# Two groups of denominator sums placed directly ahead of the key transposes in the first stage of a linear-attention and gated-FFN layer

## The chip, the cores and the metric

The kernel runs on one core of one Trainium2 chip. The metric is device time in microseconds for one execution. The engines are called PE (TensorE, with PEld for its weight loads), DVE (VectorE), ACT (ScalarE), POOL (GpSimd) and SP (SyncE, which issues the DMAs). They run in parallel, each through its own fixed queue of instructions, and meet at semaphores.

## What is computed

The input x has 4096 tokens of 512 numbers. One layer is computed, in fp32:

```python
q, k, v = x @ Wq.T, x @ Wk.T, x @ Wv.T      # 16 query heads, 4 key/value heads, 128 wide
q, k = rope(q), rope(k)
qf, kf = elu(q) + 1, elu(k) + 1
# over the tokens, for each head
state = state + kf[:, None] * v[None, :];  z = z + kf
o = (qf @ state) / (qf . z + 1e-6)
x = layernorm(x + o @ Wo.T)
x = layernorm(x + ffn(x))    # two Walsh-Hadamard transforms around a gated FFN of width 2048
```

## The kernel before

The first stage (projections and linear attention, about the first 930 us) is the only one that the change touches. It walks over 8 tiles of 512 tokens. In each tile there are 4 groups (one key head and its 4 query heads) and 4 chunks of 128 tokens. The later stages (output projection with the first layer norm, then the FFN) are left as they are.

Each engine's work in a tile is written out by hand as a list of events: one letter and two digits. A prime means that the event belongs to the next tile, so the tiles overlap. `ORDER_*` (L44 to L75) is the list of a tile in a loop over 6 tiles, run once more ahead of it as "first", `START_*` fills the pipeline and `LAST_*` (L183 to L198) is the last tile. The events that matter here:

- PE: `Jgc` projects one head (c = 0 is the key of group g, 1 to 4 its queries) with 12 matmuls of 512 columns (L626). `Vc` projects values. `Dg` sums the products q·z of a group over the partitions with a matrix of ones (L650, four fp32 matmuls that show as 8 records, each in its own quarter of the columns). `Tg` transposes the key of group g (L644, fp32). `Cgc` is the scores of a chunk (L657, 3 matmuls of 512 columns), `Zgc` adds to the state (L664, 3 matmuls of 128 columns), `Ugc` forms the numerators of a chunk (L677 and L680, 6 matmuls of 512 columns). Apart from D and T, the operands are split in two fp32r parts.
- ACT: `S` (the rotated copy, L1006 and L1007), `X` (exp, L1010), `L` (upper part of q or k, L1016), `A` (of the scores, L1036), `N` (of the state, L1041), `K` (of the transposed key, L1025), `O` (numerators out of their bank, L1045), `H` (of x, L1032).
- DVE: `M` (times cosine, L1310), `R` (rotation summed, L1314), `E` (elu + 1, L1322; after it the projection's bank is free), `Q` (running sum of the keys, L1328), `P` (q times z, L1336; it writes the four tiles `pr` that D reads), `Y` (copies D's bank out, L1361), and the lower parts `A`, `N`, `K`, `H`, `W`.
- POOL: `I` (times sine, L1482), `L` (lower part of q or k, L1485), `G` (the causal mask on the scores, two selects, L1492).
- SP: `O` stores a chunk's numerators (L1687), `Y` a group's sums (L1692), `B` loads a piece of x (L1678).

J, V, T and D share three PSUM banks, `pj0` to `pj2`, dealt out in the order in which these jobs stand in PE's list:

```python
JOBS = [e for e in EVENTS["PE"] if e[0] in "JVTD"]
def job_bank(kind, a, b=0):
    return [e[:3] for e in JOBS].index((kind, a, b)) % NB      # NB = 3
```

`jobs_before` (L164) finds the last job of the same bank and `released` (L593) waits for the step that empties it: for J that is `f_done` of its E, for V `v_lo`, for T `t_lo` (K on DVE), for D `den_free` (Y on DVE). Before the change, the jobs around D2 get these banks: J32 2, J33 0, J34 1, D2 2, J00' 0, T3 1, J01' 2, J02' 0, J03' 1. So J01' waits for Y2, and J02' for E00'.

Further waits that the steps below use: P31 waits for D2 (`dn_done`, since D2 reads `pr`); D2 for the four P of group 2; Z for N; N for the Z before; C30 for L34 on POOL; O on ACT for the store of the numerators two units back (`num_out`), because there are two buffers `no`; Y on SP for Y on DVE. On SP the tile's list is `... O20 B2' Y2 B0' O21 O22 O23 ...`, on ACT it is `... O21 O22 L34 S00' K3 N30 O23 A30 X00' S01' ...`.

Of the kernel before, what the change touches and what calls it, by code (L numbers as in the profile page):

```python
# [42 lines left out]

ORDER_PE = """  # L44
J21 U03 C11 C12 Z10 J22 J23 J24 Z11 U10 C13 U11 D1 J30 Z12 J31 C20 U12 Z13 C21 T2 U13 J32 J33 Z20 J34 Z21 C22
U20 U21 C23 D2 Z22 U22 J00' Z23 T3 U23 C30 J01' Z30 C31 C32 J02' J03' U30 J04' Z31 U31 V0' Z32 J10' Z33 C33 V1'
C00' T0' C01' U32 U33 D3 J11' J12' Z00' U00' J13' Z01' J14' U01' V2' V3' C02' C03' Z02' J20' D0' Z03' T1' U02'
C10'
"""

# [7 lines left out]

ORDER_DVE = """
N10 R20 A10 P12 E20 P13 M21 P14 R21 N11 A11 E21 Q2 M22 R22 M23 E22 R23 M24 E23 R24 N12 A12 P21 E24 A13 Y1 P22  # L60
M30 N13 P23 R30 P24 M31 A20 R31 E30 K2 E31 N20 A21 Q3 M32 R32 M33 N21 E32 R33 H0' M34 H1' A22 N22 H2' R34 E33 Y2
H3' A23 E34 N23 P31 P32 P33 M00' K3 N30 P34 R00' A30 E00' Q0' M01' A31 R01' N31 E01' M02' R02' M03' A32 E02'
R03' M04' E03' N32 R04' W0' N33 E04' M10' A33 R10' W1' E10' K0' A00' N00' A01' P01' Y3 P02' P03' M11' P04' R11'
Q1' E11' N01' M12' R12' M13' E12' N02' R13' M14' E13' R14' W2' E14' W3' A02' A03' N03' Y0' P11' K1' M20'
"""
# [117 lines left out]

LAST_PE = """
J21 U03 C11 C12 Z10 J22 J23 J24 Z11 U10 C13 U11 D1 J30 Z12 J31 C20 U12 Z13 C21 T2 U13 J32 J33 Z20 J34 Z21 C22
U20 U21 C23 D2 Z22 U22 Z23 T3 U23 C30 Z30 C31 C32 U30 Z31 U31 Z32 C33 U32 Z33 U33 D3
"""

LAST_DVE = """
N10 R20 A10 P12 E20 P13 M21 P14 R21 N11 A11 E21 Q2 M22 R22 M23 E22 R23 M24 E23 R24 N12 A12 P21 E24 A13 Y1 P22  # L190
M30 N13 P23 R30 P24 M31 A20 R31 E30 K2 E31 N20 A21 Q3 M32 R32 M33 N21 E32 R33 M34 A22 N22 R34 E33 Y2
A23 E34 N23 K3 N30 A30 A31 N31 P31 P32 A32 N32 N33 A33 P33 P34 Y3
"""

LAST_POOL = """
# [1626 lines left out]
```

## Time and profile before

| | us |
|---|---|
| median of 3 runs | 2302.26 (2300.16 to 2302.41) |
| the profiled execution | 2300.89 |
| its span, first to last instruction | 2299.1 |
| ACT busy | 1273.6 (55%) |
| POOL busy | 1128.5 (49%) |
| mean granted TensorE clock | 0.995 |

Seven of the 8 tiles have a J01' in their list: the "first" tile and the six of the loop. Their D2 begin at 122.9, 234.6, 345.6, 457.3, 568.9, 680.6 and 791.6 us, so a tile takes about 111.5 us. The last tile's D2 begins at 903.5 us.

How to read the rows: a line of the timeline has the start and the duration in us, the engine, the line of the kernel, the operation, output<-inputs, the shape and how many instructions were merged; brackets hold the idle time before it and what ended it. Matmul records overlap: one of 512 columns lasts 0.39 us, while the next starts 0.23 us later at the full clock. So starts are compared with starts.

### The profile page before, as it was taken

What the parts mean: (1) busy time and instruction counts of PE and PEld (TensorE: products, weight loads), DVE (VectorE), ACT (ScalarE), POOL (GpSimd) and SP (SyncE); (2) the same over time, 40 slices, a digit from 0 to 9 for tenths busy, and PEclk for the clock granted to TensorE, in tenths of its full rate; (3) what the DMA queues carried; (4) which work ended last, traced back from release to release, by engine and by line L of the source; (5) the groups of instructions that cost most, each with busy time, mean ns of one, the idle gap of its engine ahead of it and who ended that gap; (6) DMA issues with size and microseconds to landing.
All of it is one profiled execution on the core that took longest, in us unless ns stands there. A gap on an engine that the chain in (4) does not pass through costs nothing.

```text
span 2299.1 us, 32686 instructions
## 1 busy us (share of the span) xinstructions
PE 2255.0 (98%) x10226; PEld 1826.7 (79%) x10226; DVE 1827.3 (79%) x2479; ACT 1273.6 (55%) x2285; POOL 1128.5 (49%) x1007
## 2 busy tenths in 40 slices
PE   8899999999999999999999999999999999999998
PEld 6678787787878787788888778888888888888887
DVE  6777777778786868888888897787888788878877
ACT  6666666666666767233444455454545544554543
POOL 5667676767676767455544733321342133303321
PEclk9999999999999999999999999999999999999999
DMA  4011201111110215777778541323223322222323
GB/s 158 33 65 38 70 35 66 43 63 56 45 69 32 73 35 198 264 254 256 251 243 269 184 131 56 123 84 113 82 94 97 115 88 92 92 83 83 102 64 101
DMA packets 132710, 252.87 MB, mean 110 GB/s; under 512 B 44576, under 2 KB 45344, under 8 KB 122880
## 3 DMA queue, kind: packets, MB, share of 16 engines
q1 hardware_dynamic: 132608, 251.60, 32.7%
q8 instruction: 53, 0.87, 0.2%
q14 instruction: 49, 0.40, 0.1%
HBM read 188.11 MB, written 63.44 MB: 109 GB/s over the span
## 4 chain that ended last, share of the span: by engine, by line
PE 71%; issue 11%; POOL 10%; DVE 5%; ACT 2%; DMA 0%; POOLq 0%; ACTq 0%; DVEq 0%; SPq 0%
PE pj L626 16%; PE pj L709 10%; PE pnum L709 6%; PE pj L723 5%; PE psc L709 5%; PE pst L709 4%; PE psc L723 4%; PE pj L636 3%; PE pnum L723 3%; PE psc L657 3%; PE pnum L677 3%; PE pnum L680 3%; PE pst L723 2%; POOL fa L1415 1%; POOL fb L1416 1%
## 5 line engine op out<-in xcount | busy, mean ns | idle before, releaser
L1445 POOL TENSOR_TENSOR wcs<-wcr 128x256 f32<-128x256 f32 x64 | 67.8, 1060 | 514.7 <-DVE wcl L1187 504.3
L1482 POOL TENSOR_TENSOR tb<-tb,sinb 128x512 f32<-128x512 f32 x160 | 223.4, 1396 | 82.4 <-ACT tb L1007 82.1
L626 PE MATMUL pj<-xah,wqh 128*128 128x512 f32 x504 | 200.3, 397 | 4.0 <-DVE Kf L1322 2.4
L1485 POOL TENSOR_TENSOR Ql<-tb,Qh 128x512 fp32r<-128x512 f32 x128 | 170.9, 1338 | 66.9 <-ACT Qh L1016 66.9
L547 PE MATMUL pj<-woh,oh 128*128 128x512 f32 x512 | 202.1, 395 | 0.0
L547 PE MATMUL pj<-woh,ol 128*128 128x512 f32 x512 | 200.0, 391 | 0.0
L547 PE MATMUL pj<-wol,oh 128*128 128x512 f32 x512 | 199.8, 390 | 0.0
L626 PE MATMUL pj<-xah,wql 128*128 128x512 f32 x504 | 197.1, 391 | 0.0
L626 PE MATMUL pj<-xal,wqh 128*128 128x512 f32 x504 | 197.0, 391 | 0.0
L1310 DVE TENSOR_TENSOR pj<-pj,cosb 128x512 f32<-128x512 f32 x157 | 109.1, 695 | 77.8 <-ACT tb L1007 77.3
L1492 POOL TENSOR_SCALAR_AFFINE_SELECT Ah<-Ah 128x512 fp32r<-128x512 f32 x128 | 101.3, 792 | 113.9 <-DVE Al L1351 113.2
L709 PE MATMUL pj<-xch,wch 128*128 128x512 f32 x384 | 151.3, 394 | 5.7 <-DVE xcl L1193 3.8
L1006 ACT ACTIVATE tb<-pj 64x512 f32<-64x512 f32 x157 | 93.6, 596 | 111.0 <-PE pj L626 109.2
L709 PE MATMUL pj<-xcl,wch 128*128 128x512 f32 x384 | 150.6, 392 | 0.0
L709 PE MATMUL pj<-xch,wcl 128*128 128x512 f32 x384 | 150.4, 392 | 0.0
L1336 DVE TENSOR_TENSOR pr<-tb,zc 128x512 f32<-128x512 f32 x128 | 139.0, 1100 | 1.0 <-PE pj L650 1.0
L1314 DVE SCALAR_TENSOR_TENSOR pj<-pj,tb 128x512 f32<-128x512 f32 x157 | 108.8, 693 | 32.1 <-POOL tb L1482 31.0
L1010 ACT ACTIVATE tb<-pj,minus 128x512 f32<-128x512 f32 x157 | 108.3, 690 | 42.0 <-DVE pj L1314 40.4
L1398 POOL TENSOR_TENSOR rstd<-ve,neghalf 128x1 f32<-128x1 f32 x32 | 40.4, 1262 | 182.1 <-DVE ve L1078 182.1
L626 PEld LDWEIGHTS pj<-xah,wqh 128*128 128x128 f32 x504 | 95.3, 189 | 31.2 <-issue 5.9
L1258 DVE SCALAR_TENSOR_TENSOR tha<-tha,ga 128x512 f32<-128x512 f32 x64 | 53.6, 837 | 80.8 <-ACT tha L952 80.7
L922 ACT ACTIVATE wdh<-wdr 128x512 fp32r<-128x512 f32 x123 | 77.1, 627 | 69.0 <-PE pj L723 34.8
(291 smaller groups left out, 7110.2 us busy)
## 6 DMA issues: line engine op xcount, KB each, us to landing
num_scratch<-no SPq DMA_DIRECT2D x128, 256.0 KB, 2.4
nt<-num_scratch SPq DMA_DIRECT2D x32, 1024.0 KB, 5.5
rb<-rden_scratch SPq DMA_DIRECT2D x32, 1024.0 KB, 6.8
wdr<-wd_scratch SPq DMA_DIRECT2D x128, 256.0 KB, 3.2
wcr<-in_wg SPq DMA_DIRECT2D x64, 256.0 KB, 2.7
wcr<-in_wu SPq DMA_DIRECT2D x64, 256.0 KB, 3.1
xst<-in_xT SPq DMA_DIRECT2D x34, 256.0 KB, 3.8
xr<-in_x SPq DMA_DIRECT2D x32, 256.0 KB, 5.6
```

The lines of the kernel that those rows point to most:

```text
L547: last = nc.tensor.matmul(py[s][:, :], a[s][:, h, :], b[:, h, :], start=(h == 0 and i == 0), stop=(h == H - 1 and i == 2))
L626: last = nc.tensor.matmul(bank[:, :], w[:, b, :], x[:, b, :], start=(k == 0), stop=(k == 11))
L709: last = nc.tensor.matmul(bank[:, :], a[n % 2][:, w, c, :], b[i][:, c, :], start=(start and k == 0), stop=(k == 5), skip_group_check=True)
L723: last = nc.tensor.matmul(result_banks(k)[t][:, :], a[:, tok], b[:, :], start=(f == 0 and i == 0), stop=(f == FB - 1 and i == 2))
L1006: nc.scalar.activation(tb[c][0:64, :], bank[64:128, :], ACT.Copy)
L1010: nc.scalar.activation(tb[c][:, :], jobs_at[bank_index("J", g, c, where)][:, :], ACT.Exp, bias=minus1[:, 0:1]).then_inc(exp_done, 1)
L1310: nc.vector.tensor_tensor(bank[:, :], bank[:, :], cosb[:, :], ALU.mult).then_inc(cos_done, 1)
L1314: nc.vector.scalar_tensor_tensor(out=bank[:, :], in0=bank[:, :], scalar=1.0, in1=tb[c][:, :], op0=ALU.add, op1=ALU.add).then_inc(rot_done, 1)
L1336: nc.vector.tensor_tensor(pr[c - 1][:, :], tb[c][:, :], zc[:, :], ALU.mult).then_inc(z_product, 1)
L1482: nc.gpsimd.tensor_tensor(tb[c][:, :], tb[c][:, :], sinb[:, :], ALU.mult).then_inc(sin_done, 1)
L1485: nc.gpsimd.tensor_tensor(Ql[g % 2][:, c, :], (tb[c] if c else Kf)[:, :], f32(Qh[g % 2][:, c, :]), ALU.subtract).then_inc(lo_done, 1)
L1492: ins = nc.gpsimd.affine_select(out=a[:, :, :], in_=a[:, :, :], compare_op=ALU.is_ge, fill=0.0, base=0, pattern=[[0, G], [1, CH]], channel ...
```

## The change

In every tile D2 moves behind Z22, U22, J00' and Z23, to stand directly ahead of T3, and D0' moves behind Z03', to stand directly ahead of T1'. DVE's Y2 moves behind H3', A23, E34 and N23, since D2 now follows Z23, which needs N23. SP's, ACT's and POOL's lists stay.

```diff
 ORDER_PE
-U20 U21 C23 D2 Z22 U22 J00' Z23 T3 U23 C30 J01' Z30 C31 C32 J02' J03' U30 J04' Z31 U31 V0' Z32 J10' Z33 C33 V1'
-C00' T0' C01' U32 U33 D3 J11' J12' Z00' U00' J13' Z01' J14' U01' V2' V3' C02' C03' Z02' J20' D0' Z03' T1' U02'
+U20 U21 C23 Z22 U22 J00' Z23 D2 T3 U23 C30 J01' Z30 C31 C32 J02' J03' U30 J04' Z31 U31 V0' Z32 J10' Z33 C33 V1'
+C00' T0' C01' U32 U33 D3 J11' J12' Z00' U00' J13' Z01' J14' U01' V2' V3' C02' C03' Z02' J20' Z03' D0' T1' U02'
 C10'
 ORDER_DVE
-M30 N13 P23 R30 P24 M31 A20 R31 E30 K2 E31 N20 A21 Q3 M32 R32 M33 N21 E32 R33 H0' M34 H1' A22 N22 H2' R34 E33 Y2
-H3' A23 E34 N23 P31 P32 P33 M00' K3 N30 P34 R00' A30 E00' Q0' M01' A31 R01' N31 E01' M02' R02' M03' A32 E02'
+M30 N13 P23 R30 P24 M31 A20 R31 E30 K2 E31 N20 A21 Q3 M32 R32 M33 N21 E32 R33 H0' M34 H1' A22 N22 H2' R34 E33
+H3' A23 E34 N23 Y2 P31 P32 P33 M00' K3 N30 P34 R00' A30 E00' Q0' M01' A31 R01' N31 E01' M02' R02' M03' A32 E02'
 LAST_PE
-U20 U21 C23 D2 Z22 U22 Z23 T3 U23 C30 Z30 C31 C32 U30 Z31 U31 Z32 C33 U32 Z33 U33 D3
+U20 U21 C23 Z22 U22 Z23 D2 T3 U23 C30 Z30 C31 C32 U30 Z31 U31 Z32 C33 U32 Z33 U33 D3
 LAST_DVE
-M30 N13 P23 R30 P24 M31 A20 R31 E30 K2 E31 N20 A21 Q3 M32 R32 M33 N21 E32 R33 M34 A22 N22 R34 E33 Y2
-A23 E34 N23 K3 N30 A30 A31 N31 P31 P32 A32 N32 N33 A33 P33 P34 Y3
+M30 N13 P23 R30 P24 M31 A20 R31 E30 K2 E31 N20 A21 Q3 M32 R32 M33 N21 E32 R33 M34 A22 N22 R34 E33
+A23 E34 N23 Y2 K3 N30 A30 A31 N31 P31 P32 A32 N32 N33 A33 P33 P34 Y3
```

The order of the shared-bank jobs changes with it, from `J34 D2 J00' T3 J01' J02'` to `J34 J00' D2 T3 J01' J02'`. The code deals the banks out anew: J00' gets bank 2 and D2 bank 0. The start's list has `Z03 D0 T1` already and stays; the swap of D0' and Z03' leaves the order of the jobs as it was.

## Rows read from the trace of the kernel before

**Rows 1.** The page's first part, busy time and share of each engine.
```profile
PE 2255.0 (98%) x10226; PEld 1826.7 (79%) x10226; DVE 1827.3 (79%) x2479; ACT 1273.6 (55%) x2285; POOL 1128.5 (49%) x1007
```
**Rows 2.** Who waited for whom, PE, 72 to 900 us: total us, times, longest.
```profile
PE pnum L677 <- POOL Al L1492: 4.3, 7, 0.6
```
**Rows 3.** Timeline of PE around D2 of a middle tile (start us, duration us).
```profile
457.26 1.06 PE L650 MATMUL pj<-pr,onesd 128*32 128x512 f32 x8
458.26 0.33 PE L664 MATMUL pst<-Vh,Kth 128*128 128x128 f32 x1
...
459.43 0.47 PE L677 MATMUL pnum<-Ah,Vh 128*128 128x512 f32 x1 [0.62 <-POOL Al L1492]
...
460.89 0.39 PE L626 MATMUL pj<-xah,wkh 128*128 128x512 f32 x1
...
463.61 0.22 PE L664 MATMUL pst<-Vh,Kth 128*128 128x128 f32 x1
...
463.89 0.63 PE L644 MATMUL pj<-identb,Kf 128*128 128x128 f32 x4
464.28 0.47 PE L677 MATMUL pnum<-Ah,Vh 128*128 128x512 f32 x1
...
466.22 0.50 PE L657 MATMUL psc<-Qh 128*128 128x512 f32 x1 [0.32 <-POOL Ql L1485]
...
467.02 0.39 PE L626 MATMUL pj<-xah,wqh 128*128 128x512 f32 x1
```
**Rows 4.** Timeline of DVE, the same tile: Y2, P31 to P33, M00', R00', E00'.
```profile
459.32 0.68 DVE L1361 COPY dn<-pj 128x512 f32<-128x512 f32 x1
...
462.41 2.61 DVE L1336 TENSOR_TENSOR pr<-tb,zc 128x512 f32<-128x512 f32 x3
465.63 0.70 DVE L1310 TENSOR_TENSOR pj<-pj,cosb 128x512 f32<-128x512 f32 x1 [0.61 <-ACT tb L1007]
...
467.89 0.68 DVE L1314 SCALAR_TENSOR_TENSOR pj<-pj,tb 128x512 f32<-128x512 f32 x1
...
469.33 0.69 DVE L1322 SCALAR_TENSOR_TENSOR Kf<-tb,pj 128x512 f32<-128x512 f32 x1 [0.17 <-ACT tb L1010]
```
**Rows 5.** Timeline of SP's queue, the same tile: Y2, then the numerators from O21.
```profile
460.16 0.60 SPq L1692 DMA_DIRECT2D den_scratch<-dn  x1
...
461.94 22.30 SPq L1687 DMA_DIRECT2D num_scratch<-no  x5
```
**Rows 6.** Timeline of ACT, the same tile: O22.
```profile
463.26 0.60 ACT L1045 ACTIVATE no<-pnum 128x512 f32<-128x512 f32 x1 [2.22 <-DMA num_scratch<-no]
```
**Rows 7.** Line L1687 (numerator stores), 450 to 470 us.
```profile
DMA to landing us min/median/max: 2.4/3.3/4.4
```
**Rows 8.** Timeline of PE where it resumes after idle time, in the first 115 us.
```profile
55.37 0.45 PE L664 MATMUL pst<-Vh,Kth 128*128 128x128 f32 x1 [4.29 <-DVE Sl L1356]
...
61.27 0.50 PE L626 MATMUL pj<-xah,wqh 128*128 128x512 f32 x1
...
108.10 0.50 PE L626 MATMUL pj<-xah,wqh 128*128 128x512 f32 x1 [2.41 <-DVE Kf L1322]
...
112.41 0.53 PE L626 MATMUL pj<-xah,wqh 128*128 128x512 f32 x1
```
**Rows 9.** Windows: busy of each engine (count), granted clock, DMA share, GB/s.
```profile
58.00:60.00 2.00, 2.00 (x7) 1.52 (x6) 0.00 (x0) 0.60 (x1) 0.00 (x0) 0.50 0.00 0
```
**Rows 10.** Timeline of PE in the start, where D0 stands directly ahead of T1.
```profile
69.92 1.06 PE L650 MATMUL pj<-pr,onesd 128*32 128x512 f32 x8
70.91 0.66 PE L644 MATMUL pj<-identb,Kf 128*128 128x128 f32 x4
```
**Rows 11.** Timelines: PE D0', DVE Y0' of the tile before; POOL I00'.
```profile
410.62 1.07 PE L650 MATMUL pj<-pr,onesd 128*32 128x512 f32 x8
...
411.84 0.69 DVE L1361 COPY dn<-pj 128x512 f32<-128x512 f32 x1 [2.66 <-PE pj L650]
...
466.13 1.28 POOL L1482 TENSOR_TENSOR tb<-tb,sinb 128x512 f32<-128x512 f32 x1
```

## The prediction

> **What bounds the kernel now.** I read the busy shares first: PE is busy 98% of the span [rows 1], the other engines at most 79%. Then the waits of PE in the stretch of the seven full tiles: the only one that comes in every tile is one of 0.6 us for POOL (7 times, 4.3 us) [rows 2], and at C30 there is one of 0.3 us in some of them [rows 3]. So in this stage a microsecond put on PE, or a wait put before it, is a microsecond of the result, and there are only about 0.9 us a tile in which a move could hide. Then the timelines of one middle tile on each engine, around D2. The reader is to see in [rows 3] which of PE's waits are there already: U22 (459.43) waits 0.62 us for POOL's mask, C30 (466.22) waits 0.32 us for POOL's L34, and J01' (467.02) starts without a wait. In [rows 4]: DVE does P31 to P33 right behind N23, and finishes E00' at 469.33 + 0.69 = 470.02, which is 3.0 us after J01' has started. All seven tiles show this pattern.
>
> **The gain that is there.** D and T are the only fp32 jobs among fp32r ones, and the first matmul behind either is longer: 0.33 us for Z behind D against 0.22 us for Z behind a projection, and 0.47 us for U behind T against the usual 0.39 us [rows 3]. So a D or a T costs about 0.1 us on the way out. Directly ahead of T, as the start has it, D's way out is gone; D takes 70.91 - 69.92 = 0.99 us, as it does now (458.26 - 457.26 = 1.00), and T lasts 0.66 instead of 0.63 us [rows 10, 3]. So a pair saves 0.11 - 0.03 = 0.08 us. There are 8 pairs D2, T3 and 7 pairs D0', T1': 15 x 0.08 = 1.2 us at most, 0.05% of the time. (On the way in I take both places as equal.)
>
> **D0' behind Z03'.** PE is not made to wait: N03' is done long before: on DVE it stands ahead of Y0', and DVE idles 2.66 us between them [rows 11]. D0' and Y0' come 0.28 us later (Z03' takes 0.28 us, as 463.61 to 463.89 shows), and with them P11' and K1' on DVE. The next user of the bank, J21, has T1', U02' and C10' ahead of it, 0.4 + 9 x 0.23 = 2.4 us behind D0' (a step of 512 columns is (463.61 - 460.89) / 12 = 0.23 us, rows 3), and Y0', which starts 411.84 - 410.62 = 1.22 us after D0' and takes 0.7 us, ends 1.9 us after D0' begins, so 0.9 us after D0' is through. That is covered. Cost nothing, gain 7 x 0.08 = 0.6 us.
>
> **D2 behind J00' and Z23: PE's own time.** U22 does not start earlier because D2 is gone from before it. Its releaser is POOL's mask, which hangs on A22 and not on D2, so U22 stays at 459.43, J00' at 460.89 and Z23 at 463.61 [rows 3]. The gap that D2 filled is left empty. Behind Z23 (0.28 us) and 0.1 us for the way in, which T behind Z doesn't show and I grant D, D2 starts at 463.61 + 0.38 = 463.99, T3 at 464.98, U23 at 465.39, and C30 six steps and T's 0.1 us later, at 465.39 + 1.46 = 466.85. The 0.32 us wait for L34, with its re-entry, is absorbed. J01' could start at 466.85 + 3 x 0.23 = 467.53, 0.51 us later than now. That includes the saving at T3.
>
> **D2 behind J00' and Z23: the DVE queue.** Y2 is queued on DVE behind N23 and ahead of P31. Y0' shows that the copy starts 1.22 us after its D [rows 11]. So Y2 starts at 463.99 + 1.22 = 465.21, and P31 at 465.81, where it started at 462.41 [rows 4]. (P31 would have waited for D2 in any case.) DVE idles about 3.4 us there. Behind P31 are queued P32, P33, M00', K3, N30, P34, R00', A30 and E00'. From P31's start to E00's end the row shows 470.02 - 462.41 = 7.61 us, of which 0.61 was a wait that now is over by then. So E00' ends at 465.81 + 7.0 = 472.8.
>
> **The new wait.** Before the change nobody on PE needed E00' before J02', which stands 3 + 12 + 6 matmuls behind (Z30, J01', C31, C32), some 4 us after J01' starts. But the banks are dealt by the order of the jobs, and J00' and D2 have swapped: J01' now takes the bank of J00'. That bank is released by E00', not by Y2. J01' is ready at 467.53 and may start at 472.8: **PE waits 5.3 us**, and J01' is 472.85 - 467.02 = 5.8 us later than now. The chain is D2 on PE, Y2, three P, M00', R00', X00' on ACT, E00' on DVE, J01'. Behind J01' on PE stands the rest of the tile, and there is nothing to win it back with: PE has no other waits [rows 2]. Everything that S01' and the later steps wait for moves with PE.
>
> Bounds. The lower one: the three P took 2.61 us while POOL worked [rows 4], and other DVE steps of this shape follow each other by 0.6 us; four P at 0.6 us end the chain 0.8 to 1.0 us earlier. The Trainium skill (GPSIMD Engine Reference, Key points) says that GpSimd shares its SBUF interfaces with VectorE, with contention for VectorE instructions that have two SBUF inputs, as P has; by that rule the P that start after POOL's I00' ends (467.41, rows 11) are the short ones, and the sum would be 0.6 us a tile lower, 4 us in all. I keep the row's 7.0 us, because a second chain comes up right behind: SP. Its queue holds Y2 ahead of B0' and O21. Y2's store goes out 0.84 us after the copy starts [rows 4, 5], now at 466.05, and O21's store two issues of 0.6 us later, at 467.3 instead of 461.94. It lands 2.4 to 4.4 us later, 3.3 in the median [rows 7], so at 469.7 to 471.7. O23 on ACT waits for it as O22 now does for O20's [rows 6], and ACT does A30 and X00' only after O23. From O23 over A30 on both engines to E00's end is about 2.5 us: 472.2, 473.1 or 474.2. So J01' starts between 472.2 and 474.2, and is between 5.2 and 7.2 us late; I take 5.8, where the two chains nearly meet.
>
> **The clock after the wait.** When PE resumed after 4.29 us of idle time, it ran in the next windows at a granted clock of 0.50, with 7 matmuls in 2 us instead of 9, the level of 1.2 GHz [rows 8, 9]. Up to 61.27 it did 3 matmuls of Z and 12 of 512 columns in 5.90 us, for which the full clock needs 0.28 + 12 x 0.23 = 3.1 us: 2.8 us lost. After 2.41 us of idle time a projection job took 112.41 - 108.10 = 4.31 us, against 463.61 - 460.89 = 2.72 us: 1.6 us lost. After the 0.6 us waits nothing is lost. The new idle time of 5.3 us is longer than both, so I add 2.2 us a tile, bounds 1.6 and 2.9; and nothing, if the clock stays up.
>
> **The last tile.** No J00' and no J01'. D2 is late by about 2.8 us, behind U22 and Z23. Its 1.0 us leaves one place and comes back at the other, and no bank wait is added, since without the primed jobs T3 is the next one. I count nothing, with one D, 1.0 us, as the bound either way.
>
> **The sum**, on the profiled execution's 2300.9 us: 7 tiles x (5.8 + 2.2) = 56.0, less 0.6 for D0', T1', makes 55.4 and 2356.3 us. The median of the runs is 1.4 us above that execution, so I forecast **2357 us**, 2.4% slower. Lower end with the low clock: 7 x (5.2 + 1.6) = 47.6, 2348 us. Upper end: 7 x (7.2 + 2.9) = 70.7, 2371 us.
>
> **The rivals.**
> 1. The bank wait is there, but the clock stays at 2.4 GHz. For it: U22's and C30's waits leave the clock alone. Against it: both idle times of [rows 8] brought the low clock, and both were shorter. 7 x (5.2 to 5.8) gives 2338 to 2342 us. Chance 0.20.
> 2. The wait at J01' does not arise or is short, because E00' is done by 467.5. It would need DVE to be through 5 us earlier, against its written order. Then only D2's own shift counts: 7 x 0.51 - 0.6 = +3, 2305 us, within what can be told from no change. Chance 0.05.
> 3. On the other side: D2's old place holds U22 back, not POOL. If the mask were ready when Z22 ends early, U22 would start 1 us sooner, the 0.62 us wait would go in seven tiles and the pair would save its 0.08: 7 x 0.62 + 1.2 = 5.5 us less, 2297 us. It decides from the point where the mask is done before 458.8, and where E00' is in time. Against it: [rows 3] name POOL as the releaser, while D2 had ended. Chance 0.02.
> 4. More than the forecast: O21's late store holds ACT, then O23 and the numerator banks, and the low clock lasts longer than after the 4.29 us, or a second wait opens at J02' or U30. From 7 x 10.1 on: over 2371 us. Chance 0.08.
> The forecast itself, 2343 to 2371 us: 0.65.
>
> **How the numbers follow.** The range leaves out rival 2 and 3, most of 4 and the lowest part of 1: 2334 to 2368 us. What can be told from no change in this kernel is about 0.2%, 4.6 us. Faster by more: 0.02 (rival 3). Within it: 0.05 (rival 2). Slower by more: 0.93 (the rest).
>
> **What would show it.** In the trace of the changed kernel: U22 still waits for POOL, now about 1.7 us after Z22; Y2 on DVE with 3 us or more of idle time ended by L650; in seven tiles the first matmul of J01' with an idle time of about 5 us ended by DVE L1322 (Kf); behind it a granted clock of 0.50 for 3 to 6 us; the tile's period at 119 us; D0', T1' with no wait; the last tile as before. I am wrong if L1322 is not the releaser of J01', if the idle time there is under 3 us, or if the granted clock behind it stays at 1.00. If the idle time is ended by E00' but E00' waited for ACT, the second chain (SP, O23) was the longer one.

## The result and the profile after

The changed kernel takes 2376.83 us in the median (2374.47 to 2377.84), against 2302.41 us for the kernel before, run beside it: a ratio of 1.0323, 95% interval 1.0309 to 1.0338. That is 74 us more, where I had forecast 55 (2357 us, range 2334 to 2368). The sign was right, the size too small by a quarter. The profiled execution has a span of 2374.9 us, 75.8 us more than before.

The page's busy line, to be read against [rows 1]: PE is busy 25 us longer, although the number of its instructions is the same, and its share of the span has fallen. So there is both idle time and slower work.

```profile
PE 2279.8 (96%) x10226; PEld 1844.5 (78%) x10226; DVE 1825.6 (77%) x2479; ACT 1274.0 (54%) x2285; POOL 1121.8 (47%) x1007
```

Who waited for whom on PE, 72 to 900 us (total us, times, longest), to be read against [rows 2]:

```profile
PE pj L626 <- DVE Kf L1322: 43.5, 8, 6.0
PE pnum L677 <- POOL Al L1492: 8.5, 7, 1.2
PE pj L626 <- DVE tb L1322: 3.0, 3, 1.4
PE pst L664 <- DVE Sl L1356: 2.3, 7, 0.4
```

The first line is new. Of its 43.5 us, 2.4 us were there before the change (108.10 in rows 8); the other 41.1 us are seven waits of J01', one in each tile. The waits for POOL's mask have doubled, from 4.3 us in the old kernel to 8.5 us.

One middle tile on PE (start us, duration us, idle time before and its releaser in brackets), to be read against [rows 3]:

```profile
486.12 0.33 PE L664 MATMUL pst<-Vh,Kth 128*128 128x128 f32 x1 [0.32 <-DVE Sl L1356]
...
487.89 0.47 PE L677 MATMUL pnum<-Ah,Vh 128*128 128x512 f32 x1 [1.22 <-POOL Al L1492]
...
489.60 0.63 PE L626 MATMUL pj<-xah,wkh 128*128 128x512 f32 x1
...
494.04 1.07 PE L650 MATMUL pj<-pr,onesd 128*32 128x512 f32 x8
495.04 0.66 PE L644 MATMUL pj<-identb,Kf 128*128 128x128 f32 x4
495.45 0.48 PE L677 MATMUL pnum<-Ah,Vh 128*128 128x512 f32 x1
...
503.70 0.80 PE L626 MATMUL pj<-xah,wqh 128*128 128x512 f32 x1 [5.93 <-DVE Kf L1322]
...
508.99 0.31 PE L664 MATMUL pst<-Vh,Kth 128*128 128x128 f32 x1
```

The reader sees the predicted steps in order: U22 still waits for POOL, now 1.22 us; D2 stands at 494.04, T3 1.00 us behind it; J01' waits 5.93 us for E00' (Kf), and its 12 matmuls, of 0.63 us each but the first, take 5.29 us instead of 2.7. One thing was not predicted: J00' (489.60) already runs in matmuls of 0.63 us. The windows of the same tile (busy of PE, PEld, DVE, ACT, POOL with counts, then the granted clock) show the clock at half, 1.2 GHz, in both places (489 to 490 and 504 to 505); behind U22 it is still full in the first microsecond and falls after it:

```profile
488.00:489.00 1.00, 1.00 (x5) 0.83 (x6) 1.00 (x1) 1.00 (x4) 1.00 (x2) 1.00 0.84 262
489.00:490.00 1.00, 1.00 (x4) 0.74 (x3) 1.00 (x2) 0.51 (x2) 1.00 (x1) 0.51 0.95 354
...
496.00:498.00 2.00, 1.77 (x8) 1.13 (x6) 2.00 (x3) 0.50 (x2) 0.43 (x1) 1.00 0.02 4
...
504.00:505.00 1.00, 1.00 (x3) 0.81 (x3) 1.00 (x1) 0.00 (x0) 0.45 (x1) 0.50 0.00 0
```

DVE in the same tile, to be read against [rows 4]: Y2 waits 4.32 us for D2, and everything behind it is late. The last wait, 1.58 us ahead of A30, is for ACT.

```profile
490.67 0.28 DVE L1356 TENSOR_TENSOR Sl<-pst,Sh 128x128 fp32r<-128x128 f32 x1
495.26 0.69 DVE L1361 COPY dn<-pj 128x512 f32<-128x512 f32 x1 [4.32 <-PE pj L650]
495.87 2.31 DVE L1336 TENSOR_TENSOR pr<-tb,zc 128x512 f32<-128x512 f32 x3
498.11 0.68 DVE L1310 TENSOR_TENSOR pj<-pj,cosb 128x512 f32<-128x512 f32 x1
...
499.50 0.67 DVE L1336 TENSOR_TENSOR pr<-tb,zc 128x512 f32<-128x512 f32 x1
500.10 0.68 DVE L1314 SCALAR_TENSOR_TENSOR pj<-pj,tb 128x512 f32<-128x512 f32 x1
502.36 0.69 DVE L1351 TENSOR_TENSOR Al<-psc,Ah 128x512 fp32r<-128x512 f32 x1 [1.58 <-ACT Ah L1036]
502.97 0.68 DVE L1322 SCALAR_TENSOR_TENSOR Kf<-tb,pj 128x512 f32<-128x512 f32 x1
```

Why ACT was late stands in its own timeline and in SP's queue, to be read against [rows 5, 6]. O23 waits 4.75 us for the store of O21, which left only at 497.66, because Y2 stands ahead of it on SP:

```profile
501.25 0.60 ACT L1045 ACTIVATE no<-pnum 128x512 f32<-128x512 f32 x1 [4.75 <-DMA num_scratch<-no]
501.74 0.59 ACT L1036 ACTIVATE Ah<-psc 128x512 fp32r<-128x512 f32 x1
```
```profile
496.12 0.60 SPq L1692 DMA_DIRECT2D den_scratch<-dn  x1
497.05 0.34 SPq L1678 DMA_DIRECT2D xst<-in_xT  x1
497.66 4.68 SPq L1687 DMA_DIRECT2D num_scratch<-no  x3
```

### The profile page after: what moved, and what is told of

Its sections match the earlier page's. It is cut to its first block, busy times and chain, and to the rows that moved or that the text cites. A ratio compares the mean times of both kernels' runs of the same rounds, so it can differ in the third digit from the quotient of the medians.

```text
span 2374.9 us, 32698 instructions
## 1 busy us (share of the span) xinstructions
PE 2279.8 (96%) x10226; PEld 1844.5 (78%) x10226; DVE 1825.6 (77%) x2479; ACT 1274.0 (54%) x2285; POOL 1121.8 (47%) x1007
## 4 chain that ended last, share of the span: by engine, by line
PE 70%; issue 11%; POOL 9%; DVE 6%; ACT 2%; DMA 2%; SPq 0%; POOLq 0%; ACTq 0%; DVEq 0%
PE pj L626 17%; PE pj L709 10%; PE pnum L709 5%; PE pj L723 5%; PE psc L709 5%; PE pst L709 4%; PE psc L723 4%; PE pj L636 3%; PE pnum L723 3%; PE pnum L677 3%; PE pnum L680 3%; PE psc L657 3%; PE pst L723 2%; POOL fa L1415 1%; POOL fb L1416 1%
## 5 line engine op out<-in xcount | busy, mean ns | idle before, releaser
L626 PE MATMUL pj<-xah,wqh 128*128 128x512 f32 x504 | 207.2, 411 | 45.1 <-DVE Kf L1322 43.5
L626 PE MATMUL pj<-xal,wqh 128*128 128x512 f32 x504 | 202.6, 402 | 0.0
L626 PE MATMUL pj<-xah,wql 128*128 128x512 f32 x504 | 202.5, 402 | 0.0
L626 PEld LDWEIGHTS pj<-xah,wqh 128*128 128x128 f32 x504 | 98.4, 195 | 75.9 <-DVE Kf L1322 48.8
L1336 DVE TENSOR_TENSOR pr<-tb,zc 128x512 f32<-128x512 f32 x128 | 132.1, 1046 | 1.0 <-PE pj L650 1.0
L922 ACT ACTIVATE wdh<-wdr 128x512 fp32r<-128x512 f32 x123 | 77.1, 627 | 71.5 <-PE pj L723 34.8
```

The lines of the kernel that those rows point to most:

```text
L626: last = nc.tensor.matmul(bank[:, :], w[:, b, :], x[:, b, :], start=(k == 0), stop=(k == 11))
L1336: nc.vector.tensor_tensor(pr[c - 1][:, :], tb[c][:, :], zc[:, :], ALU.mult).then_inc(z_product, 1)
```

## The experiments

My theory: the swap of the banks makes J01' wait for E00', SP's queue lengthens that wait, idle time brings the low clock behind it, and D2's own 1.0 us has lost its cover. The rivals: DVE's order alone would hold PE whatever the bank; the low clock has another cause than the idle time; D2 had held U22 back. In each experiment the ratio is to the kernel before, run beside it. On those chips it took 2299.5 to 2300.4 us.

**The old banks.** The change, but D2 and J00' keep their banks:

```diff
 JOBS = [e for e in EVENTS["PE"] if e[0] in "JVTD"]
+JOBS.remove(("D", 2, 0, 0))
+JOBS.insert(JOBS.index(("J", 0, 0, 1)), ("D", 2, 0, 0))
```

> The change, with the three shared banks dealt as before it (D2 bank 2, J00' bank 0), so J01' waits for Y2 and J02' for E00'. If the new bank wait is what holds PE for 5.9 us a tile (my theory): J01' starts without a wait, about 3.5 us behind D2; A30, late on ACT behind O23, now holds C32 by some 1.8 us; the low clock behind J01' is gone or short. 7 x about 3.5 us plus 5 us in the last tile: about 2331 us, ratio to before about 1.013. If the queue on DVE or on SP would hold PE at that place whatever the bank: J01' or the step behind it waits as long as now and the time stays near 2377 us.

Measured: 2329.56 us against 2299.49, ratio 1.0133 (1.0117 to 1.0150). PE's waits, 72 to 900 us (its line numbers are 2 higher):

```profile
PE psc L659 <- DVE Al L1353: 11.1, 7, 1.8
PE pnum L679 <- POOL Al L1494: 8.5, 7, 1.2
```

J01' has no wait left; of the E00' line only the 2.4 us remain that were there before the change. C32 waits 1.2 to 1.75 us for A30, as expected, and no low clock follows it (behind U22 it still comes in five tiles). The bank wait and the clock behind it are worth 74.4 - 30.1 = 44 us, more than half of the loss; the 11 us of waits at C32 are left of it, and they fall to 1.9 us when SP's list is changed too, as shown below. The rival that DVE's order holds PE there by itself falls.

**SP's Y2 behind O21 and O22.** The change, with one event moved on SP:

```diff
-O20 B2' Y2 B0' O21 O22 O23
+O20 B2' B0' O21 O22 Y2 O23
```

> The change, with Y2 on SP moved behind O21 and O22, so that the store of O21 isn't queued behind the sums of D2. If O23 (waiting for O21's store) sets A30 and with it E00': the 4.75 us wait of O23 goes, E00' ends 0.8 us earlier, at 8.86 instead of 9.66 us behind D2, and the last tile loses nothing: 7 x 0.8 + 5 = 10.6 us less, about 2366 us. If the DVE queue alone sets E00': no change, 2377 us, and the last tile's 5 us stay.

Measured: 2361.89 us against 2299.49, ratio 1.0270 (1.0253 to 1.0287), so 62.4 us more than before instead of 74.4. J01' waits now 4.5 to 5.1 us instead of 5.9:

```profile
PE pj L626 <- DVE Kf L1322: 35.0, 8, 5.1
```

43.5 - 35.0 = 8.5 us of it is J01'. Another 2 us came from the last tile, where C32 waits 1.43 us for A (971.18) instead of 3.38 us (985.67). The low clock behind the shorter wait is shorter too: from J01' to J02' the seven tiles took 48.8 us in the changed kernel and take 44.8 us here. These three make 14.5 us, where the medians give 12.0. So the SP queue was the longer of the two chains, by more than the 0.8 us a tile that I gave it: 1.2 us.

**Both.**

> Both of the above. If bank and SP queue are the two causes: J01' without a wait, C32 and J02' with 0.3 us at most, the last tile as before. What is left is D2's own time on PE, 0.5 us a tile, and the low clock behind U22's longer wait, 1.6 us in about 5 tiles: 7 x 0.5 + 5 x 1.6 + 2 = 14 us, about 2316 us. If the DVE queue (Y2 and the P behind D2) is a cause of its own: 10 us or more above that.

Measured: 2313.25 us against 2299.49, ratio 1.0060 (1.0043 to 1.0077). What is left is 13.8 us, with these waits of PE:

```profile
PE pnum L679 <- POOL Al L1494: 8.5, 7, 1.2
...
PE psc L659 <- DVE Al L1353: 1.9, 5, 0.6
```

The time is the expected one (14 us), but by luck: I had put 8 us of it down to the low clock behind U22 in five tiles, and it came in one, 1.6 us. In its place stand D2's own time, which is larger than I had it (0.8 us a tile, see below), and the stretch from J01' to J02', which took 31.1 us in the seven tiles of the kernel before and takes 34.8 us here. So the bank and SP's queue are the causes of 60 of the 74 us, with the low clock that follows the wait at J01', and with some 6 us by which the low clock behind U22 came less often. DVE's new order, with the 1.9 us of waits for A30, accounts for at most 3.7 us.

**PE kept at work ahead of J01'.** The change, with 24 matmuls of other data (L626's shape) into a score bank that is free, ahead of J01'. C31 overwrites their result.

```diff
+def keep_warm(m, u, n):
+    pe.wait_ge(sc_free, upto(m, 0, NU, u - 2))
+    for _ in range(n):
+        nc.tensor.matmul(psc[u % 2][:, :], wvh[:, 0, 0:P], wvh[:, 0, :], start=True, stop=True)
 ...
+if where in ("first", "middle") and (kind, g, c, d) == ("J", 0, 1, 1):
+    keep_warm(m, 13, 24)
```

> The change, with 24 matmuls of 512 columns of other data into a score bank that is free, put on PE ahead of J01' where it idles 5.9 us (24 x 0.2275 = 5.5 us); their result is overwritten by C31. If idle time is what brings the low clock behind J01': the granted clock stays at 1.00 there, J01' and C31 take their full-clock time, 2.75 us less in each of 7 tiles, 2357 to 2358 us; J01' starts no later. If the low clock there has another cause: no change, 2377 us.

Measured: 2360.89 us against 2299.49, ratio 1.0262 (1.0245 to 1.0280), 13 us less than the change itself, though PE does 168 matmuls more. PE now idles 0.3 to 0.5 us ahead of J01' in six tiles and not at all in the first, and no matmul of J01' lasts 0.63 us. The idle time is what brought the low clock there. The saving is 6 us smaller than the 19 us that I expected. From J01' to J02' the seven tiles took 48.8 us in the changed kernel and take 32.0 us here, so 16.8 us came back; in this run the low clock behind U22 came in 6 tiles, not 5, which takes 1.6 us of it; about 2 us are not assigned.

**The same, and 4 matmuls ahead of U22.**

```diff
+if where in ("first", "middle") and (kind, g, c, d) == ("U", 2, 2, 0):
+    keep_warm(m, 12, 4)
```

> As the 24 matmuls ahead of J01', and 4 more (0.9 us) between Z22 and U22, where PE idles 1.2 us for POOL's mask. If that short idle time (with the 0.3 us ahead of Z22) brings the low clock in 5 of 7 tiles: D2 comes 4.56 us behind U22 in all tiles instead of 6.15, 5 x 1.6 = 8 us less than with the 24 alone, about 2350 us. If not: as with the 24 alone.

Measured: 2352.52 us against 2299.95, ratio 1.0230 (1.0214 to 1.0246). PE's wait for the mask shrinks to 0.2 us:

```profile
PE pnum L686 <- POOL Al L1501: 1.7, 7, 0.3
```

From U22 to D2 it is 4.55 us in all seven tiles, and no full-size matmul of the seven tiles from U22 on lasts 0.63 us. So the short wait of U22 does bring the low clock, and the clock in both places cost 74.4 - 52.6 = 22 us (25.0 us between the spans of the two traces, 2374.9 and 2349.9). Rival 1, a clock that stays up, is out.

**D2 one step later, behind U22.** The kernel before, with D2 moved past Z22 and U22 only; the order of the bank jobs stays:

```diff
-C23 D2 Z22 U22 J00' Z23 T3        (PE)      -E33 Y2 H3' A23 E34 N23 P31  (DVE)
+C23 Z22 U22 D2 J00' Z23 T3                  +E33 H3' A23 E34 N23 Y2 P31
-O20 B2' Y2 B0' O21 O22 O23        (SP)
+O20 B2' B0' O21 O22 Y2 O23
```

> The kernel before with D2 one step later in the loop's tiles, behind Z22 and U22 instead of ahead of them (banks unchanged, as the jobs keep their order; Y2 behind N23 on DVE and behind O22 on SP, as in the kernel with old banks and the SP list changed). It takes away only the work that hid POOL's mask. If the mask sets U22 whatever PE does before it: U22 waits 1.2 us as in the changed kernel, and D2's 1.0 us comes on top, less what C30's wait takes: 7 x 0.5 = 3.5 us, and 1.6 us for each tile in which the low clock follows: 2303 to 2312 us. If D2 had held U22 back: 2 us or more less than before.

Measured: 2311.76 us against 2300.37, ratio 1.0052 (1.0035 to 1.0069). U22 waits 1.22 us:

```profile
350.04 0.33 PE L664 MATMUL pst<-Vh,Kth 128*128 128x128 f32 x1 [0.32 <-DVE Sl L1356]
351.81 0.48 PE L677 MATMUL pnum<-Ah,Vh 128*128 128x512 f32 x1 [1.22 <-POOL Al L1492]
```

The mask sets U22, not D2: taking D2 away from before it wins nothing, and D2 has to be paid at its new place. From one U22 to the next it takes 112.25 us in tiles without the low clock, against 111.42 us on average before, so the lost cover costs 0.8 us a tile, not the 0.5 us that I had worked out. With the low clock in two tiles (1 and 4) that makes 8.8 of the 11.4 us; the rest is not assigned. This move alone makes the kernel slower.

**The last tile alone.** The kernel before, with only the two `LAST` lists changed:

> The kernel before, with the change made in the last tile's lists alone (D2 and Y2). My prediction's term: 0, within 1.0 us. The trace of the changed kernel says: O23 waits 1.9 us for a store queued behind Y2 on SP, A30 and A31 come late and C32 waits 3.4 us: about 5 us, 2307.5 us, ratio 1.002.

Measured: 2303.37 us against 2299.95, ratio 1.0015 (1.0006 to 1.0025): 3.4 us, less than the 5 us that I expected, since C32 had waited 0.84 us for A before the change already. From D1 to D3 of the last tile it takes 52.77 us, against 50.56 us in the kernel before: 2.2 us. The trace shows the expected chain. SP issues Y2 at 908.34 and O21 behind it, O23 on ACT waits for that store, and C32 on PE (914.60) waits 3.34 us for A:

```profile
908.34 0.58 SPq L1692 DMA_DIRECT2D den_scratch<-dn  x1
908.97 0.44 SPq L1687 DMA_DIRECT2D num_scratch<-no  x1
```
```profile
912.64 0.60 ACT L1045 ACTIVATE no<-pnum 128x512 f32<-128x512 f32 x1 [1.80 <-DMA num_scratch<-no]
```

**The second move alone.** The kernel before, with D0' and Z03' swapped:

> The kernel before, with D0' and Z03' swapped alone. My prediction's term: 0.08 us less in each of 7 tiles, 0.6 us less, 2301.7 us, ratio 0.9997. If entering D or T costs as much as leaving it, or Y0' 0.3 us later is felt: within 0.5 us of no change or above. The row to read is PE's from J20' to C10' in each tile: 0.08 us shorter.

Measured: 2300.23 us against 2299.95, ratio 0.9999 (0.9990 to 1.0008). The time can't tell 0.6 us from nothing, but the trace can: from the last matmul of J20' to the first of U02' it takes 412.24 - 410.24 = 2.00 us, against 412.38 - 410.30 = 2.08 us in the kernel before.

```profile
410.24 0.39 PE L626 MATMUL pj<-xah,wkl 128*128 128x512 f32 x1
410.46 0.22 PE L664 MATMUL pst<-Vh,Kth 128*128 128x128 f32 x1
...
410.84 1.06 PE L650 MATMUL pj<-pr,onesd 128*32 128x512 f32 x8
411.83 0.66 PE L644 MATMUL pj<-identb,Kf 128*128 128x128 f32 x4
412.24 0.48 PE L677 MATMUL pnum<-Ah,Vh 128*128 128x512 f32 x1
```

**Two second profiles**, to see whether the length of U22's wait decides on the low clock.

> The changed kernel as it is, for a second profile. If the low clock behind U22's wait is set by that wait's length: the same 5 of 7 tiles have it. If it also hangs on when in time the wait falls: another count. Behind J01' (5.9 us) all 7 tiles have it in either case.

> The kernel with the old banks and SP's Y2 late, for a second profile: the same U22 wait of 1.2 us with the low clock in 1 of 7 tiles. If the length of the wait sets it, 1 of 7 again; if it hangs on the moment, another count, and a time that differs by 1.6 us for each.

Measured: 2376.62 us and 2315.29 us. In the changed kernel U22 to D2 took 6.15 us (low clock) or 4.55 us (full clock). In the first profile the low clock came in tiles 1, 3, 4, 6 and 7, in the second in tiles 1, 2, 4, 5 and 7: again five, but not the same ones. In the kernel with old banks and SP changed, it came in tile 1, and the second time in tiles 1 and 7. The wait was 1.16 us in tile 1 and 1.22 us in the others every time, as in these two rows of the changed kernel's second tile, where the clock stayed up:

```profile
245.22 0.47 PE L677 MATMUL pnum<-Ah,Vh 128*128 128x512 f32 x1 [1.22 <-POOL Al L1492]
...
249.76 1.06 PE L650 MATMUL pj<-pr,onesd 128*32 128x512 f32 x8
```

So its length alone doesn't decide. The kernels in which a second wait of over 1 us stands in each tile (J01' or C32), or the 24 matmuls in its place, had it in 5 or 6 of 7 tiles; those without it (old banks and SP changed, twice, and D2 behind U22) in 1 or 2. But that second wait can't decide alone either: in the changed kernel it stands in every tile, and in its tile 2 the low clock stayed away in the first profile and came in the second, with the same work and the same waits ahead of U22. What is left of what I can name is the moment at which the wait falls. The start has another such case: the wait of 2.41 us from [rows 8] stands in all twelve traces, 2.38 to 2.42 us long, with the low clock behind it in ten. In the changed kernel's first profile the clock stayed up:

```profile
107.62 0.50 PE L626 MATMUL pj<-xah,wqh 128*128 128x512 f32 x1 [2.41 <-DVE Kf L1322]
...
110.48 0.39 PE L626 MATMUL pj<-xah,wqh 128*128 128x512 f32 x1
```
```profile
110.00:112.00 2.00, 2.00 (x10) 1.66 (x9) 1.90 (x3) 1.19 (x2) 2.00 (x2) 1.00 0.12 44
```

The 12 matmuls took 110.48 - 107.62 = 2.86 us, against 4.31 us in [rows 8]. No run sets the moment on purpose, so that it decides is argued and not shown.

## Why the prediction was wrong in size

The forecast's main path was right and is shown: the swap of the banks, E00' as the releaser of J01', and the low clock behind it. Two terms that it put at nothing, and three sizes, made up the rest. By its steps:

- **The gain.** Right, 0.08 us a pair: the trace of the second move alone shows it, and in the changed kernel it is 1.00 us from D2 to T3 and 0.41 us from T3 to U23, against 0.99 us from D0 to T1 in [rows 10].
- **D0' behind Z03'.** Right: nothing waits.
- **U22 stays with POOL's mask.** Right, by the kernel with D2 behind U22. Rival 3, that D2 held U22 back, is out.
- **D2's own time on PE, 0.51 us a tile.** Too small. I worked it out on a tile in which C30 had a wait to give back, and only 4 of the 7 tiles have one (in the timelines of the kernel before; rows 3 show one of them). The experiment gives 0.8 us, 2 us more in all.
- **The bank wait, 5.3 us.** The step was right: the releaser, the place and the seven tiles. The wait is 5.9 us, 41.1 instead of 37 us in all. I had put the two chains side by side and then taken the DVE chain's value, with the words that they nearly meet. SP's chain was the longer one: DVE was through P34 and R00' at 500.78, and A30 came at 502.36. J01' started 9.66 us after D2; the prediction has 472.85 - 463.99 = 8.86 us. I should have taken the later of the two chains. SP's change gave back 1.2 us a tile of it.
- **The P at their new place.** The three P took 2.31 us, against 2.61 us [rows 4], and P34 took 0.67 us. POOL's I00' ended at 496.4, during the first of them, so POOL was idle beside P34; before the change P34 ran beside I00' and took 0.91 us. The Trainium skill (GPSIMD Engine Reference, Key points) has this contention for VectorE instructions with two SBUF inputs, and the trace agrees: 0.67 us against 0.91 us. With it DVE's chain from P31 to E00' was 503.65 - 495.87 - 1.58 = 6.2 us and not 7.0, as the prediction's lower bound has it; that saved nothing, since SP's chain was the longer.
- **The clock behind J01', 2.2 us.** Right in kind, a little small. From J01' to J02' it took 6.5 to 7.3 us, 48.8 us in the seven tiles, against 31.1 us before: 17.7 us, 2.5 us a tile. 77 of the 512-column matmuls, at 0.2 us each, are 15 us of it. One of the two idle times that this step rests on, 2.41 us, doesn't bring the low clock every time, as shown above; those of 5.5 us and more did.
- **The clock behind U22: the step that failed.** The prediction says "After the 0.6 us waits nothing is lost", and goes on with the wait at J01' only. But it had said itself that the gap D2 filled stays empty, and its signs have U22 1.7 us after Z22, so the wait was no longer 0.6 us. It was 1.22 us, with 0.32 us more ahead of Z22 and three short matmuls between them. It brought the low clock in 5 of 7 tiles, 1.6 us each, 8 us.
- **The last tile, 0 within 1.0 us: the other step that failed.** I looked at PE and at banks there and not at SP's queue, though I had named that very queue for the other tiles. It cost 3.4 us by the time (between 1.4 and 5.8 us by the interval), 2.2 us by the trace.
- **Rival 4, over 2371 us, chance 0.08.** Its time came, and its mechanism in part: O21's late store held O23 and with it J01'. The low clock behind J01' was not longer than its bounds, and no second wait opened at J02' or U30. What carried the time past 2371 us stands in no rival: the clock behind U22 and the last tile.

The sum by these terms, in the trace: 41.1 (J01') + 17.7 (clock behind it) + 8 (clock behind U22) + 5.6 (D2's cover, 7 x 0.8) + 2.2 (last tile) - 0.6 = 74.0 us, of the 75.8 us by which the span grew. That it comes so near is partly luck, since parts that the change doesn't touch differ between the two traces: the first tile's U22 starts at 122.92 instead of 125.03, and what stands behind the last D3 takes 2.7 us longer. Against the 55.4 us of the forecast, 8 and 2.2 us are the two terms put at nothing, 6.1 us the wait and D2's cover (46.7 us instead of 7 x 5.8), and 2.3 us the clock behind J01'.

The experiments leave no version that beats the kernel before. Old banks, SP's Y2 late and D2 at its new place cost 14 us, and the harmless half of the change gains 0.6 us, which the time can't show.

## What to carry to other kernels

Where buffers are dealt by the position of their jobs in a list, moving one job changes who waits for whom among jobs that were not moved; write out the table of buffers before and after, and price each new pair by the step that releases it. When a short job leaves a gap that another engine's wait had kept open anyway, nothing is won at the old place, the whole job is paid at the new one, and the gap it leaves can cost more than its length. Follow the moved step's output on every queue, in the first and last pass too: here a store that had to wait for its data (Y2, 496.12) held the one queued behind it on SP, and through it ACT, DVE and PE.

## What the runs showed of the hardware

A TensorE wait of 1.2 us, with one of 0.3 us and three short matmuls just before it, was enough to bring the granted clock from 2.4 to 1.2 GHz for about seven 512-column matmuls, at a price of 1.6 us, more than the wait itself. It did so in 5 of 7 tiles of one kernel, twice, and in 1 and then 2 of 7 of another, with the same wait. Waits of 0.6 us at that place never did, in the 7 tiles of the kernel before. A wait of 2.4 us in the start brought it in ten of twelve traces. Behind idle times of 5.5 to 6.1 us the clock was low in 7 of 7 tiles in both profiles, for 9 to 12 such matmuls. Matmuls of unrelated data put into the idle time kept it up, and the kernel was faster for doing more work: 1.0230 times the kernel before against the change's 1.0323, with 196 matmuls more.
